# A windowed-attention and ternary-FFN layer on one core: four PSUM banks in one rotation, finer waits in the FFN, normalisations on GpSimd

## The reference

```python
x = x + attn(layernorm(x), Wq, Wk, Wv, Wo)     # 16 heads of 16, softmax over the last 64 keys
x = x + ffn(layernorm(x), W1, b1, W2, b2)      # h = relu(xn @ T(W1).T + b1); h @ T(W2).T + b2
def layernorm(x): return (x - mean(x)) / sqrt(var(x) + 1e-5)
def T(W):         return clip(round(W / (mean(abs(W)) + 1e-5)), -1, 1)
```

## Time and profile before

| | us |
|---|---|
| median of three runs | 808.15 (807.88 to 808.19) |
| the profiled execution | 808.77 |
| its span | 807.0 |
| PE busy | 710.5 (88%) |
| PEld (weight loads) busy | 592.8 (73%) |
| DVE busy | 701.4 (87%) |
| ACT busy | 659.9 (82%) |
| POOL busy | 517.0 (64%) |

### The profile page before, as it was taken

The page is one execution under the profiler, slowest core; times in us unless marked ns, Lnnn a source line. Parts: engine busy times, 40 slices in busy tenths (PEclk is TensorE's granted clock), DMA queues, the critical chain, the costliest instruction groups (busy, mean ns, idle before and its releaser), DMA issues.

```text
span 807.0 us, 25066 instructions
## 1 busy us (share of the span) xinstructions
PE 710.5 (88%) x8370; PEld 592.8 (73%) x8370; DVE 701.4 (87%) x1632; ACT 659.9 (82%) x2708; POOL 517.0 (64%) x660
## 2 busy tenths in 40 slices
PE   4728669999999999999999999989999999999696
PEld 2516558878778787878778787878878787878575
DVE  4636999999999999999999999999999999898853
ACT  2558769989898989989898989889898989899822
POOL 6445576767666766767676766767676766667710
PEclk9877979999999999999999999999999999999999
DMA  3864523526263543626262544526262444533000
GB/s 127 184 91 93 67 43 25 103 28 105 55 93 69 66 98 30 127 32 103 53 102 60 66 101 34 120 31 103 54 100 60 40 101 31 97 36 63 15 28 27
DMA packets 430760, 57.69 MB, mean 71 GB/s; under 512 B 403364, under 2 KB 422182, under 8 KB 430632
## 3 DMA queue, kind: packets, MB, share of 16 engines
q1 hardware_dynamic: 421128, 45.86, 38.3%
q10 hardware_dynamic: 9504, 10.22, 4.1%
HBM read 12.00 MB, written 8.39 MB: 25 GB/s over the span
## 4 chain that ended last, share of the span: by engine, by line
ACT 39%; DVE 25%; issue 19%; PE 6%; POOL 6%; SPq 3%; DMA 1%; DVEq 0%; ACTq 0%; POOLq 0%
ACT p L369 22%; ACT th L378 6%; DVE negm L540 5%; DVE xnC L635 4%; SPq L206 3%; DVE hTl L650 3%; PE ps L884 2%; POOL tl L301 2%; DVE pt L553 2%; ACT oTh L422 2%; ACT hTh L433 2%; ACT xTCh L427 2%; ACT osum L415 2%; POOL p L292 2%; ACT xTAh L384 2%
## 5 line engine op out<-in xcount | busy, mean ns | idle before, releaser
L369 ACT ACTIVATE p<-ps,negm 128x96 f32<-128x96 f32 x1024 | 338.4, 358 | 83.7 <-DVE negm L540 82.2
L301 POOL TENSOR_TENSOR tl<-pt,th 128x384 f16<-128x384 f32 x256 | 241.6, 944 | 154.4 <-ACT th L378 153.0
L292 POOL TENSOR_TENSOR p<-p,rden 128x384 f32<-128x384 f32 x256 | 212.0, 828 | 45.1 <-DVE rden L547 45.0
L369 ACT ACTIVATION_READ_ACCUMULATOR p<-ps,negm 128x1 f32 x1024 | 229.7, 224 | 0.0
L540 DVE TENSOR_REDUCE negm<-ps 128x4 f32<-128x384 f32 x256 | 138.4, 541 | 10.6 <-PE ps L774 10.4
L553 DVE STREAM_TRANSPOSE pt<-p 128x384 f32<-128x384 f32 x256 | 140.7, 549 | 2.4 <-POOL p L292 1.9
L378 ACT ACTIVATE th<-pt 128x384 f16<-128x384 f32 x256 | 141.4, 552 | 0.3 <-DVE pt L553 0.3
L774 PEld LDWEIGHTS ps<-k,qbd 128*128 128x128 f16 x2048 | 119.0, 100 | 26.8 <-issue 2.2
L774 PE MATMUL ps<-k,qbd 128*128 128x96 f16 x2048 | 132.8, 209 | 0.0
L884 PE MATMUL ps<-w2T,hTl 128*128 128x256 f16 x512 | 115.2, 273 | 0.0
L884 PE MATMUL ps<-w2T,hTh 128*128 128x256 f16 x512 | 115.2, 272 | 0.0
(11 more groups left out here) (106 smaller groups left out, 1365.3 us busy)
## 6 DMA issues: line engine op xcount, KB each, us to landing
k<-kst SPq DMA_DIRECT2D x64, 288.0 KB, 3.8
qbd<-qs SPq DMA_DIRECT2D x256, 32.0 KB, 2.1
vb<-vd SPq DMA_DIRECT2D x256, 32.0 KB, 2.5
out<-x SPq DMA_DIRECT2D x32, 256.0 KB, 3.1
x<-in_L_attn_hidden ACTq DMA_DIRECT2D x15, 512.0 KB, 4.8
vb<-in_L_ffn_W ACTq DMA_DIRECT2D x2, 1024.0 KB, 9.2
x<-in_L_attn_hidden SPq DMA_DIRECT2D x1, 512.0 KB, 4.6
x<-in_L_attn_Wo ACTq DMA_DIRECT2D x1, 256.0 KB, 5.9
```

Of the source, the lines that this page charges most:

```text
L292: e.tensor_tensor(p3, p3, rden[n % 4][:, :].unsqueeze(2).to_broadcast([128, 4, 96]), ALU.mult).then_inc(s_nm, 1)
L301: e.tensor_tensor(tl[g % 2][:, o], pt[n % 3][:, :], th[g % 2][:, o], ALU.subtract).then_inc(s_lo, 1)
L369: ins = e.activation(p[:, 96 * u:96 * u + 96], bank[:, 96 * u:96 * u + 96], ACT.Exp, bias=m[:, u:u + 1], accum_out=r[:, u:u + 1])
```

## The change

Three things are changed together.

1. Banks 4 to 7 are one rotation. A new table, TURN, walks over all uses of stages A and C in the order in which TensorE issues them and gives each the next of the four banks and the name of its last holder; uses in slots below 24 go on alternating over banks 4 and 5, as banks 6 and 7 hold the ternary weights' transposes until then. TensorE waits for that holder's VectorE operation, of stage A or of stage C (`free`). ScalarE and VectorE look up the bank in the same table.
2. `c_f` waits for the high part of its input before the first matmul, and for the low part only ahead of the first matmul that reads it. `c_y` now sums over the eight blocks' high parts first and then over their low parts, and waits ahead of each second block for the piece it reads.
3. `a_norm` and `c_norm` are on GpSimd, with the same operands. In a slot GpSimd issues `rstd_c`, `rstd_a`, `carry`, `low`, then `c_norm`, then `norm`, then `a_norm`. Stage A's slots go from (-6, -5) to (-8, -7) relative to the chunk, that is from slots 10 and 11 to slots 8 and 9.

```diff
-A_STATS, A_RSTD, A_NORM = (-13, -12), -10, (-6, -5)
+A_STATS, A_RSTD, A_NORM = (-13, -12), -10, (-8, -7)
...
+    turn, holder, nxt = {}, {}, 0
+    for slot, _, _, stage, c, name in sorted(order):
+        nxt = nxt + 1 if slot >= 24 else (nxt + 1) % 2
+        bank = 4 + nxt % 4
+        turn[stage, c, name] = bank, holder.get(bank)
+        holder[bank] = stage, c, name
...
 # gpsimd
+            def c_norm(c, u):
+                h = 2 * c + u
+                e.wait_ge(s_rsC, h + 1)
+                if h >= 1:
+                    e.wait_ge(s_c, USE[(h - 1) // 2, f"t{(h - 1) % 2}"] + 1)
+                for t in range(2):
+                    ins = e.tensor_scalar(xnC[:, t, :], xs[c % NX][:, 2 * u + t, :], mvC[u][:, t, 0:1],
+                                          rstdC[u][:, t:t + 1], ALU.subtract, ALU.mult)
+                ins.then_inc(s_xnC, 1)
...
                 if 0 <= n - 4 < NQ:
                     low(n - 4)
+                for u in range(2):
+                    c = stage_c(n, C_NORM[u])
+                    if c is not None:
+                        c_norm(c, u)
                 if 0 <= n - 2 < NQ:
                     norm(n - 2)
+                for u in range(2):
+                    c = stage_a(n, A_NORM[u])
+                    if c is not None:
+                        a_norm(c, u)
...
 # tensor
+            def free(stage, c, name):
+                bank, held = TURN[stage, c, name]
+                if held is None and bank < 6:
+                    e.wait_ge(s_wlo, 6)
+                elif held is None:
+                    e.wait_ge(s_td, 8)
+                elif held[0] == "A":
+                    e.wait_ge(s_alo, 8 * held[1] + held[2] + 1)
+                else:
+                    e.wait_ge(s_cdv, USE[held[1:]] + 1)
+                return banks[bank]
...
             def c_f(c, h, f):
-                bank = c_bank(USE[c, f"f{h}{f}"])
-                e.wait_ge(s_cdv, USE[c, f"t{h}"] + 1)
+                bank = free("C", c, f"f{h}{f}")
+                e.wait_ge(s_chi, SPLIT[c, f"t{h}"] + 1)
...
                     for xp in range(2):
+                        if xp:
+                            e.wait_ge(s_cdv, USE[c, f"t{h}"] + 1)
...
             def c_y(c, h, t):
-                w = USE[c, f"y{h}"]
-                bank = c_bank(w)
-                e.wait_ge(s_cdv, USE[c, f"f{h}3"] + 1)
+                bank = free("C", c, f"y{h}")
...
-                for f in range(8):
-                    for hp in range(2):
+                for hp, done, count in ((0, s_chi, SPLIT), (1, s_cdv, USE)):
+                    for f in range(8):
+                        if f % 2 == 0:
+                            e.wait_ge(done, count[c, f"f{h}{f // 2}"] + 1)
```

More of the change, by code:

```diff
@@ L162, in build, with a_bank, c_bank @@
         below = xnC[:, :, :].rearrange("p a b -> p (a b)")
+        def a_bank(c, w):
+            return banks[TURN["A", c, w - 8 * c][0]]
+        def c_bank(c, name):
+            return banks[TURN["C", c, name][0]]
         block = ctx.enter_context(nc.Block())
@@ L590, in a_k @@
                 e.wait_ge(s_ahi, w + 1)
-                e.scalar_tensor_tensor(out=lo, in0=abank[w % 2][:, :], scalar=1 / WS, in1=hi,
+                e.scalar_tensor_tensor(out=lo, in0=a_bank(c, w)[:, :], scalar=1 / WS, in1=hi,
                                        op0=ALU.mult, op1=ALU.subtract).then_inc(s_alo, 1)
@@ L627, in c_stats @@
                 ins.then_inc(s_mvC, 1)
[L629 to L637, removed]
             def c_t(c, h):
-                w = USE[c, f"t{h}"]
                 e.wait_ge(s_chi, SPLIT[c, f"t{h}"] + 1)
-                e.tensor_tensor(xTC[1][:, :, :].rearrange("p a b -> p (a b)"), cbank[w % 2][:, :],
+                e.tensor_tensor(xTC[1][:, :, :].rearrange("p a b -> p (a b)"), c_bank(c, f"t{h}")[:, :],
                                 xTC[0][:, :, :].rearrange("p a b -> p (a b)"),
@@ L712, in _ @@
                         c_stats(c, u)
[L713 to L717, removed]
-                    if c is not None:
-                        a_norm(c, u)
                 gg = group_at(n, PV_LAG + 2)
@@ L811, in a_qk @@
             def a_qk(c, t, n):
-                w = 8 * c + 2 + 4 * t + "qk".index(n)
-                bank = a_bank(w)
+                bank = free("A", c, (2, 6)[t] + "qk".index(n))
                 e.wait_ge(s_alo, 8 * c + 2)
@@ L823, in a_v @@
             def a_v(c, u):
-                bank = a_bank(8 * c + 4 + u)
+                bank = free("A", c, 4 + u)
                 for t in range(2):
@@ L833, in a_v @@
                 ins.then_inc(s_a, 1)
-            def c_bank(w):
-                if w >= 2:
-                    e.wait_ge(s_cdv, w - 1)
-                else:
-                    e.wait_ge(s_td, 8)
-                return cbank[w % 2]
             def wo(c, u):
+                bank = free("C", c, f"wo{u}")
+                e.wait_ge(s_td, 8)
                 e.wait_ge(s_olo, 2 * c + 2)
-                bank = c_bank(USE[c, f"wo{u}"])
                 for t in range(2):
@@ L856, in c_t @@
                 e.wait_ge(s_xnC, 2 * c + h + 1)
-                bank = c_bank(USE[c, f"t{h}"])
+                bank = free("C", c, f"t{h}")
                 for k in range(2):
```

81 lines of the change are left out of this document (37 added, 44 removed).

## The result

| | before | after |
|---|---|---|
| median, us | 808.17 (807.88 to 808.83) | 846.17 (844.39 to 847.06) |
| ratio to before | | 1.0466 (95%: 1.0446 to 1.0486) |
| profiled execution, its span | 808.77, 807.0 | 844.39, 842.6 |
| one period | 45.24 | 47.89 |

The change costs 38 us. The prediction was 776, faster.

The account below looks back on a forecast made before the run. No single engine bounds: TensorE, VectorE and ScalarE, almost full, hold each other up, VectorE late. Period 45.24 to 43.3 gives 27.3 us, tail 5, start zero: 808.8 − 32.3 = 776.5, so 776; range 765 to 798.

Parts of the forecast that it names:

- I take 0.50: One normalising instruction of 256 elements on GpSimd was priced at 0.50 us, like the conversion; eight a period add 4.0.
- the upper end of 0.94: Highest price for one normalising instruction on GpSimd, 0.94 us, a little over a 0.87 product beside other work.
- The break-even: Length of one GpSimd normalising instruction at which slot 11's `th` is as late as before: 1.35 us.
- The slower rival: GpSimd's path from statistics over `rstdC` and `xnC` to `p` delays VectorE: about 825 us at 2.0 an instruction, chance 0.06.
- T = 1.35 to 1.5: T is one GpSimd normalising instruction: at 1.35 `th` is as late as before, from about 1.5 the period exceeds 45.24.
- The 2.1 us a period: TensorE idle time to be shed by finer FFN waits and four banks: 1.2 + 0.2 + 0.7 of its 2.48.
- The lockstep rival: ScalarE and VectorE in lockstep are the bound, TensorE's waits only move: 787 us; chance 0.28, shared with dear instructions or added waits.
- mostly met: Slot 17's wait for f2's low part, 4.9 us, passes to `xnA`'s transpose 0.46 us later, so hardly costs there.
- the 5 I took: Gain in the tail, 5 us, from both `c_y` waits and f2's two-bank waits going, out of 6.4 idle.
- their bound of 15 us: Some 50 added TensorE waits a period at 23 ns at most: 1.1 a period, 15 us; counted at nothing.
- the transpose's new wait: VectorE's transpose `pt` was to stand idle for GpSimd's `p`, some 1.8 us a period.
- the three signs: Wrong if `xnC` takes over 0.9, TensorE's idle time returns before the mask matmul, or the period is above 44.

Follow-up runs that it names:

- with constants: The changed kernel with mean and reciprocal deviation replaced by constants 0 and 1 in the 128 GpSimd instructions, against the kernel before: 841.54 us, ratio 1.0392.
- the one with all 128 instructions in other places: The changed kernel with `xnA` singly in slots 7, 8, 12, 13 and `xnC` pairs behind `p`, against the kernel before: 811.72 us, ratio 1.0041.
- the kernel with 128 columns: The changed kernel with each GpSimd normalising instruction cut to 128 of 256 columns, same places, against the kernel before: 794.64 us, ratio 0.9825.
- an instruction of 0.58 us: The changed kernel with each GpSimd normalising instruction cut to 64 of 256 columns, same places, against the kernel before: 778.49 us, ratio 0.962.
- the kernel with other places: The changed kernel with `xnA` in pairs in slots 7 and 12 and `xnC` behind `p`, against the kernel before: 823.48 us, ratio 1.0175.

## Why the prediction was wrong

**The step "I take 0.50" failed, and its bounds with it.** The instruction takes 1.22, above the upper end of 0.94. By its length at three widths it is 0.37 us + 3.33 ns an element: (1222 − 796)/128 = 3.33, (796 − 582)/64 = 3.34, 582 − 64 × 3.33 = 369. The nearest row was chosen by "streams one tensor", the conversion at 0.80 ns an element. Streaming is not what it pays for: one step of arithmetic takes 0.85 for 256, the second adds 1.07 − 0.85 = 0.22 with constants, and per-partition operands another 0.15. The two-input product of the earlier trace rows at 1.57 ns an element was the better guide, counted once for each step: 2 × 256 × 1.57 = 0.80, and the first bound I should have drawn. Even that is short of 1.22 by 0.42.

The 1.22 of the trace after is 3.2 times the fastest `xnC` of before, 0.385. "GPSIMD Engine Reference" (key points) of the Trainium skill has about 2; this case's 1.22 goes beyond it, and its rule for one-input operations (4.1, roughly line rate), to which I gave more weight, does not hold for this instruction. The rule of 2 at least pointed to the side on which I was wrong.

**The break-even failed too, and it cost more than the length.** The slower rival had the right path, "Everything queued behind `xnC` there waits, and VectorE waits for `p`", but I had it decide from T = 1.35 to 1.5. Put into that rival's own working, 1.22 gives a transpose at 432.95 + 2.44 + 0.83 = 436.22 and a `th` 0.24 earlier than before: about no loss in slot 10. Measured, the break-even for the whole change is near 0.89, and 1.22 costs 38 us. The sentence that fails is that slots 8 and 9 "take `xnA` behind `p`, where nothing but the next `tl` is queued". That looked at one slot. Two pairs in two slots running are 4.9 us of work put into a queue that has 0.9 free a slot. Behind the first pair stand `tl`, `p` and the second pair, and behind that `rstdC`, `tl`, `xnC` and `p`, so slot 10 starts late before `xnC` adds its 2.44. The kernel with only `xnA` on GpSimd shows it by itself (+2.8% over parts 1 and 2), and the one with all 128 instructions in other places gives 34 us back.

The low clock stretch is a third part which I did not foresee. After 4.11 us without work TensorE runs 4.00 us at 0.59, and a period later, after 4.10 us, it runs 4.00 at 0.61. That is at most 4.00 × 0.41 = 1.6 us a period, an estimate from the window; the period grew by 2.65. How much of the 1.6 is on the path was not isolated, since no kernel had the wait without the clock. Over 130 to 740 us the mean clock is 1.00 in the kernel with 128 columns, where TensorE's longest wait for `xnC` is 1.8 us; it is 0.98 with only `xnC` on GpSimd (2.5 us) and 0.97 in after (4.3 us) and with constants (3.6 us). So in these kernels the mean falls between the instruction of 0.80 and that of 1.07, where the time rises most. Whether the clock is the reason for that steep rise stays open.

**Parts 1 and 2: the mechanism partly right, the sum not.** The waits of `c_y` for `hTl` and of `wo` for `x` are gone, as said. The 2.1 us a period put on them did not come while VectorE was full: the period of the kernel with parts 1 and 2 alone is 45.23. The lockstep rival is right for them ("TensorE's waits only move"): 30.9 us of TensorE's waits stand in that kernel where 33.5 stood. The wait that was to be "mostly met" at `xnA`'s transpose is 4.0 us there, of 4.9. The tail did give 6.4 against the 5 I took. The added waits did not cost their bound of 15 us: the kernel that has them without the rotation takes 0.9984 of the time before. TensorE's idle time did not return before the mask matmul either, 7.3 us in the whole run against 5.6.

**What held.** With an instruction of 0.58 us the rest of the sum nearly comes out: 778.5 for the 776 forecast. By the three marks its span is 30.1 us shorter than before: the start is 0.4 longer, the middle 24.2 and the tail 6.3 shorter, where the prediction, with a slightly later cut between middle and tail, had 0, 27.3 and 5. It has a period of 377.66 − 334.51 = 43.15 for 43.3, ScalarE's wait for the row maximum 18.1, well under half of 60.5, and the transpose's new wait 27.7/14.3 = 1.9 a period for 1.8. TensorE is busy 591.4 of the 610 us from 130 to 740, 97% where I said 98 to 99. Once VectorE has room, TensorE's waits do come off, in part at least: parts 1 and 2 give 2.3% on top of part 3 and 0.8% without it. The load forecast for VectorE, 37.6 a period, is 37.54 in after. What GpSimd's own operations get back by the move, which the sum left out, is next to nothing: `p` takes 825 ns for 828. The start of the changed kernel was not zero but +4.0: two pairs of `xnA`, 2.44 and 2.42 us, stand on GpSimd close ahead of the first `veC`. The first `xnC` and TensorE's longest wait for it, 9.5, come behind that mark and so count in the middle's +33.0.

Two of the three signs that the prediction named against itself came true: `xnC` takes over 0.9, and the period is above 44.

## What to carry to other kernels

Price a new operation by what it computes, steps and operands each, not by the nearest row of the same shape, and where no row shows it let the upper bound be wide enough to change the sign. On a queue with little room in each slot (0.9 us here), write down two or three slots in a row, with every instruction behind the moved one: work in pairs cost more here than the same work singly, though its own result was not wanted for long. A wait removed on one engine while another is full moves; remove load from the full engine first, with the smaller and less urgent part of its work.

## What the runs showed of the hardware

- GpSimd, two-step scalar operation of float32 with per-partition operands: 0.58, 0.80 and 1.22 us at 64, 128 and 256 columns. Constants in place of the operands: 1.07 at 256. One step: 0.85 with a constant, 0.92 with an operand. Two-input product of 512 elements: 1.04. VectorE does the two-step operation of 256 in 0.385 at the least.
- ScalarE does the same normalisation of 256 columns as scale and bias in 0.60 us, the bias made beforehand by one small VectorE instruction.
- GpSimd's own operations gained next to nothing when VectorE's scalar operations went: `p` 828 to 825 ns. GpSimd's `xnC` itself hardly varies (1216 to 1236 ns in the kernel with other places), where VectorE's ran from 385 to 1080.
- TensorE, after standing for 4.11 us, worked the next 4.00 at a granted clock of 0.59, where the 4.00 behind these had 1.00. A period later, after 4.10 us, it was 0.61.
